# Statistics in pairs of tiles, a factor chain of four steps and a tighter load plan in a streaming normalise-project-gate kernel

## What is computed

```python
def reference(x, W, b):
    g = group_norm(x, groups=32, eps=1e-5)        # mean and variance of 4 channels x 65536 pixels
    u = mean(g, axis=1); s = sqrt(var(g, axis=1, ddof=1))
    n = einsum('bchw,oc->bohw', (g - u) / (s + 1e-6), W) + b
    return x + g * n
```

## Time and profile before

| | us |
|---|---|
| median of 3 runs | 1874.91 (1874.62 to 1876.18) |
| the profiled execution's own time | 1874.49 |
| its span, first to last instruction | 1872.7 |
| busy: PE, DVE | 1694.3, 1694.4 |
| busy: ACT, POOL | 1481.5, 1456.2 |
| mean DMA rate | 356 GB/s |

### The profile page before, as it was taken

The page is one execution under the profiler, slowest core; times in us unless marked ns, Lnnn a source line. Parts: engine busy times, 40 slices in busy tenths (PEclk is TensorE's granted clock), DMA queues, the critical chain, the costliest instruction groups (busy, mean ns, idle before and its releaser), DMA issues.

```text
span 1872.7 us, 67650 instructions
## 1 busy us (share of the span) xinstructions
PE 1694.3 (90%) x28706; PEld 917.6 (49%) x28706; DVE 1694.4 (90%) x2000; ACT 1481.5 (79%) x2634; POOL 1456.2 (78%) x1684
## 2 busy tenths in 40 slices
PE   0079999999999999999999999999999999999998
PEld 0045555555555555555555555555555555555553
DVE  5678898999989998999989999899999999888887
ACT  5689997888878887898879889788887988744442
POOL 0068788888888888888888887888887888888885
PEclk9999999999999999999999999999999999999999
DMA  9989999999999999999999999999999999854775
GB/s 375 409 315 362 369 366 336 394 391 399 365 330 416 383 396 349 356 414 384 385 339 396 396 391 374 326 409 390 392 354 356 416 376 391 302 214 183 271 267 219
DMA packets 183037, 667.33 MB, mean 356 GB/s; under 512 B 20560, under 2 KB 20944, under 8 KB 182736
## 3 DMA queue, kind: packets, MB, share of 16 engines
q1 hardware_dynamic: 109008, 394.54, 57.3%
q10 hardware_dynamic: 73728, 268.47, 35.7%
HBM read 394.49 MB, written 268.44 MB: 354 GB/s over the span
## 4 chain that ended last, share of the span: by engine, by line
PE 59%; DVE 15%; DMA 7%; issue 6%; POOL 5%; ACT 4%; SPq 2%; ACTq 0%; POOLq 0%; DVEq 0%
PE proj_ps L768 35%; PE sums_ps L756 14%; PE factor_ps L742 11%; DVE scaled L667 5%; DMA tiles<-x 4%; DVE bn L712 4%; DVE bn L713 4%; DMA out<-tiles 3%; SPq L432 2%; POOL tiles L477 2%; DVE tiles L681 2%; POOL tiles L466 1%; ACT unused L534 1%; ACT squares L594 1%; POOL sum_sq L491 0%
## 5 line engine op out<-in xcount | busy, mean ns | idle before, releaser
L768 PE MATMUL proj_ps<-scaled,w_t 128*32 128x512 f32 x8192 | 985.0, 598 | 0.1
L477 POOL TENSOR_SCALAR tiles<-tiles,columns_sb 128x1024 f32<-128x1024 f32 x512 | 575.6, 1124 | 225.6 <-DVE tiles L681 221.3
L681 DVE SCALAR_TENSOR_TENSOR tiles<-proj_ps,columns_sb,tiles 128x1024 f32<-128x1024 f32 x512 | 643.5, 1257 | 70.8 <-PE proj_ps L768 69.4
L534 ACT ACTIVATE unused<-tiles,bn 128x1024 uint8<-128x1024 f32 x560 | 635.1, 1134 | 0.0
L466 POOL TENSOR_SCALAR tiles<-tiles,columns_sb 128x1024 f32<-128x1024 f32 x512 | 618.5, 1208 | 14.8 <-DMA tiles<-x 13.8
L667 DVE TENSOR_TENSOR scaled<-tiles,factor_ps 128x1024 f32<-128x1024 f32 x512 | 619.0, 1209 | 9.6 <-PE factor_ps L742 5.5
L594 ACT ACTIVATE squares<-tiles 128x1024 f32<-128x1024 f32 x512 | 537.6, 1050 | 68.8 <-PE sums_ps L756 32.2
L756 PEld LDWEIGHTS sums_ps<-tiles,const_sb 128*32 128x32 f32 x8192 | 245.0, 110 | 310.5 <-issue 264.6
L768 PEld LDWEIGHTS proj_ps<-scaled,w_t 128*32 128x32 f32 x8192 | 213.5, 109 | 360.6 <-issue 306.5
L742 PE MATMUL factor_ps<-pieces,pick_sb 128*128 128x128 bf16 x4096 | 317.3, 220 | 69.5 <-DVE scaled L667 53.0
L756 PE MATMUL sums_ps<-tiles,const_sb 128*32 128x128 f32 x8192 | 318.8, 273 | 7.4 <-ACT squares L594 7.1
(11 more groups left out here) (58 smaller groups left out, 769.4 us busy)
## 6 DMA issues: line engine op xcount, KB each, us to landing
tiles<-x SPq DMA_DIRECT2D x752, 512.0 KB, 8.9
out<-tiles ACTq DMA_DIRECT2D x512, 512.0 KB, 7.1
const_sb<-const SPq DMA_DIRECT2D x1, 86.0 KB, 2.0
scaled<-w SPq DMA_DIRECT2D x1, 64.0 KB, 2.1
scaled<-ident SPq DMA_DIRECT2D x1, 64.0 KB, 2.1
pick_sb<-pick SPq DMA_DIRECT2D x1, 8.0 KB, 1.8
columns_sb<-bias SPq DMA_DIRECT2D x1, 0.5 KB, 2.1
```

The lines of the kernel that those rows point to most:

```text
L477: nc.gpsimd.tensor_scalar(place(s), place(s), 1.0, out_shift[:, 0:1], ALU.mult, ALU.add).then_inc(finished, 1)
L534: nc.scalar.activation(unused[:, which, :], data, (ACT.Identity, ACT.Square)[which], bias=pivot_of(of), scale=-1.0, accum_out=act_sums[:, ...
L681: nc.vector.scalar_tensor_tensor(out=place(s), in0=proj_ps[:, s % 2, :], scalar=gate_shift[:, 0:1], in1=place(s), op0=ALU.add, op1=ALU.mul ...
L768: mm = nc.tensor.matmul(proj_ps[q:q + 32, s % 2, h:h + BANK], w_t[:, q:q + 32], scaled[:, s % 2, h:h + BANK], start=True, stop=True)
```

## The change

Seven things change together.

- **Pairs.** An ACT pass covers two tiles (`low` and `high`, 2048 columns), so a pair of tiles takes two passes instead of four. 46 tiles of a normal period are ACT's (46 passes) and 18 are DVE's.
- **Phases.** ACT's passes stand at phases 0, 1 and 2 only; steps 1, 20 and 38 get two. DVE's tiles stay at phase 3, now two at a time in three places (steps 3, 19 and 39).
- **Chain.** It takes four steps: variance at phase 0, root at 1, reciprocal and POOL's correction at 2 (`LAG_INVERSE`), fit and split at 3; spread, projection, gate, finish and store each come one step later (`LAG_STORE` = 11). The factor lives in `var`, so the variance of a set waits for the pieces of the last one.
- **Order on ACT.** No pass stands before the square of the sum (`SUM_SQ_AFTER` = 0), and none between the two pieces.
- **Plan.** `STATS_LEAD` 2 to 1, `STORE_STEPS` 2 to 1, buffers in the order `ORDER`. Kept tiles (34), `LEAD` and `LOAD_GAP` stay.
- **Second batch.** `plan_filling` no longer gives tiles back to ACT.
- **act_done** counts passes of a pair.

```diff
-STATS_DVE = 24
+STATS_DVE = 18
-GIVEN_BACK = 4
-CHAIN_STEPS = 3
+ACT_PHASES = (0, 1, 2)
+CHAIN_STEPS = 4
-LAG_ROOT, LAG_FIT = LAG_VAR + 1, LAG_VAR + 2
+LAG_ROOT, LAG_INVERSE, LAG_FIT = LAG_VAR + 1, LAG_VAR + 2, LAG_VAR + 3
-STATS_LEAD = 2
-STORE_STEPS = 2
+STATS_LEAD = 1
+STORE_STEPS = 1
...
-    passes = 2 * (slots - dve)
-    at = [PIVOT_STEP + 1 + p * (until - PIVOT_STEP - 1) // passes for p in range(passes)]
-    begun += [(at[p] + 0.5, "act", at[p:p + 2]) for p in range(0, passes, 2)]
+    passes = slots - dve
+    free = [t for t in range(PIVOT_STEP + 1, until) if t % SPLIT in act_phases]
+    at = [free[p * len(free) // passes] for p in range(passes)]
+    begun += [(at[p] + 0.5, "act", at[p:p + 2]) for p in range(0, passes, 2) for _ in range(2)]
...
-        factor = sum_sq
+        factor = var
...
-        SUM_SQ_AFTER = 1
+        SUM_SQ_AFTER = 0
...
-                for i, which in todo[:count]:
-                    data = wait_stats_data(act, n, i)
-                    a = of.index[i]
+                for a, which in todo[:count]:
+                    for i in of.pairs[a]:
+                        wait_stats_data(act, n, i)
+                    low, high = sorted(places.buffer["stats", i] for i in of.pairs[a])
...
-                    nc.scalar.activation(unused[:, which, :], data, (ACT.Identity, ACT.Square)[which], bias=pivot_of(of),
+                    nc.scalar.activation(unused[:, :, :], tiles[:, low:high + 1:high - low, :],
+                                         (ACT.Identity, ACT.Square)[which], bias=pivot_of(of),
...
                         nc.scalar.activation(piece[:, :], factor[:, :], ACT.Identity, scale=at["rows_bc"]).then_inc(piece_a_done, 1)
-                        statistics(b + 1, step, of, 1)
                         act.wait_ge(rest_done, done)
...
                         dve.wait_ge(var_sum_done, ready)
+                        if ready > 1:
+                            dve.wait_ge(pieces_done, ready - 1)
...
-                    if (ready := set_behind(step, LAG_ROOT, b, own, before)) is not None:
+                    if (ready := set_behind(step, LAG_INVERSE, b, own, before)) is not None:
                         dve.wait_ge(root_eps_done, ready)
                         nc.vector.reciprocal(approx[:, :], approx[:, :]).then_inc(approx_done, 1)
```

More of the change, by code:

```diff
@@ L92, in plan_statistics @@
         begun.append((step, "dve", [step]))
-    passes = 2 * (slots - dve)
-    at = [PIVOT_STEP + 1 + p * (until - PIVOT_STEP - 1) // passes for p in range(passes)]
-    begun += [(at[p] + 0.5, "act", at[p:p + 2]) for p in range(0, passes, 2)]
+    passes = slots - dve
+    free = [t for t in range(PIVOT_STEP + 1, until) if t % SPLIT in act_phases]
+    at = [free[p * len(free) // passes] for p in range(passes)]
+    begun += [(at[p] + 0.5, "act", at[p:p + 2]) for p in range(0, passes, 2) for _ in range(2)]
     begun.sort()
     return Plan(begun)
+ORDER = [(p + 36) % BUFFERS for p in range(BUFFERS)]
 class Places:
@@ L158, in free @@
     def free(self, kind, i):
-        found = [p for p in range(BUFFERS) if min(self.room(p, (kind, i))) >= 0]
+        found = [p for p in ORDER if min(self.room(p, (kind, i))) >= 0]
         assert found, (kind, i, self.span[kind, i])
@@ L176, in predecessors, with plan_filling @@
             yield other, -int((start - o_start) // self.slots) if other != tenant else 1
[L179 to L191, removed]
+def plan_filling(plan, until, latest):
+    return Plan([(None, "dve", [min(steps[0], latest)]) if engine == "act" and steps[-1] < until else (None, engine, steps)
+                 for engine, steps in zip(plan.engine, plan.steps)])
 class Plan:
@@ L200, in __init__, with at, passes_at @@
         self.bn_slots, self.act_slots = self.engine.count("dve"), self.engine.count("act")
-    def at(self, step, engine):
-        return [(i, p) for i, steps in enumerate(self.steps) if self.engine[i] == engine
-                for p, t in enumerate(steps) if t == step]
+        act = [i for i, engine in enumerate(self.engine) if engine == "act"]
+        self.pairs = [tuple(act[a:a + 2]) for a in range(0, self.act_slots, 2)]
+    def at(self, step):
+        return [i for i, steps in enumerate(self.steps) if self.engine[i] == "dve" and step in steps]
+    def passes_at(self, step):
+        return [(a, which) for a, (i, _) in enumerate(self.pairs)
+                for which, t in enumerate(self.steps[i]) if t == step]
 def norm_gate_kernel(nc, x, w, bias, const, pick, ident, out):
@@ L216, in norm_gate_kernel @@
     assert slots * SLOT == pixels
-    plan = plan_statistics(slots, STATS_DVE, STATS_UNTIL, range(3, SPLIT))
-    first_plan = plan_statistics(slots, FIRST_DVE, STATS_UNTIL, range(SPLIT))
+    plan = plan_statistics(slots, STATS_DVE, STATS_UNTIL, (3,), ACT_PHASES)
+    first_plan = plan_statistics(slots, FIRST_DVE, STATS_UNTIL, range(SPLIT), range(SPLIT))
     assert len(plan.begin) == len(first_plan.begin) == slots
-    second_plan = plan_filling(plan, FILL_STEPS, FILL_DVE_UNTIL, GIVEN_BACK)
+    second_plan = plan_filling(plan, FILL_STEPS, FILL_DVE_UNTIL)
     places = Places(slots, kept_slots, streamed_slots, plan)
@@ L230, in act_before @@
     def act_before(n):
-        return sum(2 * plan_of(m).act_slots for m in range(n))
+        return sum(plan_of(m).act_slots for m in range(n))
     with ExitStack() as ctx:
@@ L254, in norm_gate_kernel @@
         bn = sb("bn", [P, 2 * second_plan.bn_slots, 6])
-        act_sums = sb("act_sums", [P, 2, max(plan.act_slots, first_plan.act_slots)])
+        act_sums = sb("act_sums", [P, 2, max(len(plan.pairs), len(first_plan.pairs))])
         gn = sb("gn", [P, 16])
@@ L500, in period @@
                 for step in steps(own, before, nxt):
-                    root_of = set_behind(step, LAG_ROOT, b, own, before)
+                    root_of = set_behind(step, LAG_INVERSE, b, own, before)
                     fit_of = set_behind(step, LAG_FIT, b, own, before)
@@ L588, in period @@
                     if nxt:
-                        todo.extend(of.at(step, "act"))
+                        todo.extend(of.passes_at(step))
                     if own:
@@ L708, in period @@
                     if nxt:
-                        for i, _ in of.at(step, "dve"):
+                        for i in of.at(step):
                             data = wait_stats_data(dve, b + 1, i)
```

14 lines of the change are left out of this document (7 added, 7 removed).

## The result

The changed kernel takes 1921.93 us (1917.14 to 1925.0, 5 runs) against 1874.91 us (1874.23 to 1877.85): 1.0247 times as long, 95% interval 1.0232 to 1.0263. The forecast was 1897 us, range 1840 to 1914: the direction held, the size did not. The profiled execution took 1920.42 us.

The account below looks back on a forecast made before the run. PE's steps of 3.28 us (209.9 us a period) plus waits, together 219.7, were taken as the bound. Five full periods +17.5, first -0.2, seventh +1.5, last +2.1, pipeline +2.4: +23.3 on 1874.49, so 1897 us, range 1840 to 1914.

Parts of the forecast that it names:

- What the change removes: Six of a period's nine places with two DVE tiles go, 6 x 0.82 = -4.9 us a period.
- step 63: At the period's end, the wait for late pieces at this step loses 0.5 of its 1.5 us.
- ACT's passes: On ACT, a pair's pass takes 1.98 us; 91 us a period against 90, so no gain in sum.
- the rival with ACT as the bound: Pass takes 2.26 us, pieces 0.3 to 0.4 late in each of 14 sets: 1936 us, chance 0.13.
- The 0.6 us: Late pieces where ACT has two passes in a step: +0.6 us at each of steps 20 and 40.
- The tighter plan: Loads have three steps, not four: +5.0 us at steps 56 to 60, +2.3 and +0.5 at 2 to 5.
- the queue for step 56: Three loads in a row after stream tile 57's wait; statistics tile 63 comes 3.2 us after ACT wants it.
- the walk of the period's end: Steps 56 to 60: slot 60's store, load, norm and pieces make step 60's spread 6.0 us late, taken as 5.0.
- First and seventh period: First full period -0.2 us, at 223.2; the seventh, followed by steps without statistics, +1.5 us.
- Last period and pipeline: Last period, without statistics, +2.1 us from slot 60 only; one more pipeline step, fill and drain, +2.4 us.
- In time: Stores and loads land within three steps, 9.8 us for both together: 1843 us, chance 0.27.
- The transfers' rate: Transfers at the mean rate of 377 GB/s are the bound, only the pipeline's 2.4 us added: 1877 us, chance 0.10.

Follow-up runs that it names:

- 3 room: Changed kernel with 32 kept tiles, STORE_STEPS = 2, STATS_LEAD = 2 and LOAD_GAP = 0.62: 1862.25 us, 0.9931 of the kernel before.
- 7 half stores: Changed kernel with each store writing only the first 512 of its tile's 1024 columns, plan and waits kept: 1866.02 us, 0.9957 of the kernel before.
- 10: Changed kernel with 30 kept tiles, STORE_STEPS = 3, STATS_LEAD = 2, LOAD_GAP = 0.60 and `moments` moved between the two pieces: 1852.57 us, 0.9879 of before.
- experiment 1: Kernel before with only STATS_LEAD and STORE_STEPS set from 2 to 1: 1913.55 us, 1.0204 of the kernel before.
- 11: Changed kernel with only the kept tiles cut from 34 to 32, stores still planned at one step: 1890.93 us, 1.0083 of the kernel before.
- experiment 13: Changed kernel with only SyncE's queue reordered, statistics loads 59 to 61 ahead of tile 54's load, 62 and 63 ahead of tile 57's: 1919.0 us, 1.0228 of before.
- experiment 6: Changed kernel with the edits of 3 room and `moments` moved between the two pieces: 1856.06 us, 0.9898 of the kernel before.

## Why the forecast had the direction and missed the size

Excess over 3.28 us a step, mean of periods 1 to 5, worked out from the starts of the spreads:

| steps | before | forecast | after | 3 room | 7 half stores | 10 |
|---|---|---|---|---|---|---|
| 3 to 8 | 1.6 | 3.6 | 3.7 | 1.3 | 2.2 | 1.3 |
| 16 to 44 (after: 20, 24, 40) | 5.0 | 2.8 | 3.3 | 3.3 | 3.3 | 3.3 |
| 52 to 60 | 1.5 | 5.6 | 5.8 | 0.9 | 1.4 | 1.0 |
| 61 | 0.2 | 0.2 | **2.0** | 1.6 | 1.6 | 0.2 |
| 62, 63, 0, 1 | 1.9 | 1.4 | 1.4 | 1.4 | 1.4 | 1.4 |
| sum | 10.3 | 13.7 | 16.2 | 8.6 | 9.9 | 7.3 |

- **What the change removes**: right. Six double places went, 0.82 each; step 63 fell from 1.52 to 1.02 as forecast.
- **ACT's passes**: right. The profile's page has `L538 ... 128x2048` at a mean of 1991 ns, forecast 1.98 us, so the rival with ACT as the bound falls. The 0.6 us that were to be added at each of steps 20 and 40 were 0.8 to 0.9 (the first of them appears at step 24).
- **The tighter plan**: right in mechanism, and the sum of steps 52 to 60 nearly right by luck. Store and load together took more than the planned distance leaves them; experiments 1, 3, 7 and 11 show it from four sides. But the forecast put all 5.0 us on step 60. Measured, step 60 has 2.9 and the steps before it 2.8, 2.0 of them at 55 and 56, where the forecast had about 0.6 in all: one term is too large and another is missing, and they cancel. Also, the working named the queue for step 56, and experiment 13 shows that the order in the queue is not what costs: with another order the same time is lost at other steps.
- **The step that failed** is the walk of the period's end. It followed the pieces of step 59 only to the spread of step 60 and stopped. `moments`, which follows them on ACT, was never costed: the timeline has it at 2.6 us, and with a chain of four steps it stands between piece b and the square of the next set's sum. That is 1.3 us a period (experiment 6 against 3), and 1.8 in the mean of periods 1 to 5 with the clock's part. Over the seven periods of the profiled execution step 61 has 13.2 us more than the 0.24 a period of before: 9 of them are `moments`, the rest goes with the clock. The profiled time was missed by 22.6 us (45.9 measured, 23.3 forecast), and this is the largest part of it.
- **The clock** was missing from the forecast. A term was priced as the length of its wait; behind a long one PE also runs at 1.2 GHz for a while. Period 2, the only one of 1 to 6 without such a stretch, has 14.4 us of excess, the others 14.7 to 19.8. How much of this is the clock and how much the longer wait before it, the runs leave open.
- **First and seventh period.** Forecast -0.2 and +1.5, measured +8.4 and +5.3. The first has 3.2 us at step 61, 3.8 at 56 and 57 (mean 1.4), and 6.7 at the following steps 4 and 5, twice the mean; the granted clock is 0.51 from 299 to 305 us and 0.52 from 333 to 339, at just these two places. The forecast gave it the same transfers as the others; its longer waits are seen, their cause was not tried.
- **Last period and pipeline.** Forecast +4.5, measured +2.5. Without statistics loads the stream tiles landed in time.
- **The rivals.** "In time" at 1843 is what experiment 10 nearly reaches (1852.57), once the room is there; with the planned distance of three steps it did not hold. It needed 9.8 us for a store and a load together; for slot 60 in period 2 they took 10.6. Around it, first the eleven stores from 716 us on, then the last seven stream loads:

```profile
DMA to landing us min/median/max: 2.6/5.9/8.4
```

```profile
DMA to landing us min/median/max: 3.5/4.3/6.4
```

The medians make 10.2 us (the working took 12.4, from before), the maxima 14.8. The Trainium skill's "DMA: Bandwidth & Descriptors", section "Anatomy of one DMA", has a formula, for GpSimd's path, by which both together are estimated at 6.4. Only the shortest rows, 2.6 and 3.5, come near.

- **The transfers' rate** as the bound falls too: experiment 10 moves the most bytes and is the fastest.

## What to carry to other kernels

A plan in steps is a promise about latency: before tightening it, compare its shortest distance from store to next use, in microseconds, with the loaded transfers of the trace, not with lone ones. Here one step less cost 38 us (experiment 1), and two kept tiles fewer, with stores planned at two steps again, gave back 60 (experiment 3), because the rate was not the limit. When a chain is moved by a phase, walk every engine's list on to the next thing that must be on time, through the rare operations too: those that run once a period stand somewhere else in relation to the chain afterwards.

## What was not expected of the hardware

- Behind a wait of PE of 3.71 us the granted clock stood at 0.50 in a 4 us window, and a step took 6.07 us for 3.28. In the profiled executions, before the change the mean clock was 1.000, after it 0.986; with half stores or room it is 0.997. Filling 2 us of the wait with matmuls raised it to 0.992 to 0.995, at a cost wherever PE was not waiting.
- Halving the stores' bytes shortened the loads as well, from 9.0 to 7.1 us in the median, though the loads' own bytes stayed the same. What a load takes here depends on what the stores beside it move.
